# Merged weights of a gated graph network: split halves turned by DMA in place of whole float32 products

## The chip, the cores and the metric

The kernel runs on one core of a Trainium2 chip. The metric is device time in microseconds (us). PE is the matrix engine (TensorE), PEld its weight loads, DVE VectorE, ACT ScalarE, POOL GpSimd, SP the engine that issues most transfers; SPq and ACTq are the queues of DMA-issuing instructions of SP and ACT.

## The reference, cut to what matters

There are B = 16 graphs of N = 512 nodes with D = 128 features. The first part is a gated graph network of L = 5 layers, the same GRU weights in each layer and one `weight[l]` per layer:

```python
for l in range(5):
    m = einsum('bnd,de->bne', h, weight[l])
    agg = einsum('bij,bid->bjd', A, m)
    h = _gru_cell(agg, h, w_ih, w_hh, b_ih, b_hh)   # gi = agg @ w_ih.T + b_ih
x = _layernorm(x + h * mask)
```

The second part is a small graph convolution over the first 25 nodes in five groups, with a softmax of five weights, then another residual and layernorm. It is spread through and behind the first part and matters here only by the tile BD, which holds its block-diagonal adjacency.

## The kernel before, in words

**The merged weights.** The aggregation works on h itself, and `weight[l]` is multiplied into `w_ih` once: WC[l] is `weight[l] @ w_ih.T`, 128 x 384, kept as two float16 halves (high and low part) scaled by 1024. Every float32 product of the network is made of three float16 matmuls: high by high, high by low, low by high (split_product, L783 to L786).

**The steps.** The work is 80 steps k = 0 to 79, one graph and one layer each, in an order written out by hand (ROUNDS, GRAPH, LAYER). Layer 1 appears first at step 4, layer 2 at step 10, layer 3 at step 17, layer 4 at step 25. PE runs, for step k: the aggregation of the *next* step k + 1 (aggregate, L779, 8 matmuls), the gates from the state (gates_of_state, 9 matmuls), then between(k), then the gates from the messages (gates_of_messages, 9 matmuls: R, Z, then IN). In steps 1 and 2 the aggregation of step k + 1 comes last instead of first, so that those of steps 3 and 4 lie next to each other. gates_of_messages waits for wc_lo at the first step of a layer, so step 4 needs WC[1]. ACT makes in each step the high half of the messages (L1145), issues loads, makes the high half of the new state (L1149), then the gates R and Z and the tanh. DVE makes the new state (L1399, L1403), the low half of the messages (L1383), the candidate (L1389, L1393), then prepare(k). POOL makes the low half of the state (state_lo, L526), the kept share Z * H (kept_share, L515), then its own prepare(k). Each engine runs its instructions in the order of the code.

**The turned states.** The aggregation of step t needs the state in natural layout, NAT, which SP makes from the transposed state HT by one DMA transposition of both halves, 128 x 1024 float16 (transpose(t), L400 to L414). SP issues them one behind the other in the order t = 2, 4, 3, 5, 6, ... (L454); the transposition for step 5 waits for the aggregation of step 3 and for the low half of the state of step 1. In the first layer of a graph the same transposition goes from NAT to HT.

**The merge before.** w_ih is turned by PE at the start and stored as WIT; weight[0] too, and WC[0] is merged at once. At step 2, between(2) turns weight[1] to weight[4] by four float32 PE transposes into bank pC (L1000), and DVE's prepare(2) copies the bank to WLT (L1541). At steps 3, 4, 5, 6 between(k) runs merge(k - 2): one float32 matmul with 384 columns (L763, shown by the profile as two), from which ACT takes the high half before its R of the same step (L1138) and DVE the low half in prepare(k) (L1363). All these weights lie in scr, a view of BD; so POOL's prepare(7) waits until the five merges are done and then zeroes BD (L657) and H1 (L658). POOL's prepare(16) (L673 to L675) and DVE's work on degrees follow a chain of their own in steps 13 to 22, which fills BD.

**The loads.** ACT issues in step k, behind the high half of the messages, the loads that tables give: adjacency matrices of 1 MB (load_a, L1116), states x (L1090); in step 3 the matrix of graph 4, in steps 4 to 7 a small corner of all adjacencies (L1097), in step 4 also the matrix of graph 5.

Of the kernel before, what the change touches and what calls it, by code (L numbers as in the profile page):

```python
# [6 lines left out]
ALU = mybir.AluOpType  # L7
ACT = mybir.ActivationFunctionType
# [8 lines left out]
L = 5  # L17
# [11 lines left out]
WARM_UP = 6  # L29
WSCALE = 1024.0  # L30
UNSCALE = 1.0 / WSCALE


ROUNDS = [(0, 1, 2, 3),
# [94 lines left out]
def graph_net_kernel(nc, x, adj, nodemask, weight, w_ih, w_hh, b_ih, b_hh, W1, b1, W2, b2, fusion_w, out):  # L129
    ctx = ExitStack()  # L130
    with ctx:
# [6 lines left out]
        def sem(name):  # L138
            return ctx.enter_context(nc.semaphore(name))
# [66 lines left out]
        WL = scr[:, 6 * D:11 * D].rearrange("p (l e) -> p l e", l=L)  # L206
        WT = scr[:, 11 * D:15 * D]
        WIT = WT[:, 0:3 * D]
        WLT = scr[:, 14 * D:19 * D].rearrange("p (l e) -> p l e", l=L)


        y_flat = Y[:, :, :, :].rearrange("p s i d -> p (s i d)")
# [81 lines left out]
        wh_lo = sem("wh_lo")  # L294
        wi_t = sem("wi_t")
        wi_v = sem("wi_v")
        wl_t = sem("wl_t")
        wl_v = sem("wl_v")
        wc_mm = sem("wc_mm")
        wc_hi = sem("wc_hi")  # L300
        wc_lo = sem("wc_lo")
# [86 lines left out]
        @block.sync  # L388
        def _(sp):
            def load_x(b):  # L390
                if b >= 3:

                    sp.wait_ge(nat_lo, b - 2)
                    sp.wait_ge(x_t, b - 2)
                sp.dma_start(XS[:, b % 3, :, :], x[b, :, :].rearrange("(i p) d -> p i d", p=P)).then_inc(ld_x[b % 3], 16)

            def load_a(b):
                sp.dma_start(AS[:, b % 3, :, :], adj[b, :, :].rearrange("(i p) n -> p i n", p=P)).then_inc(ld_a[b % 3], 16)

            def transpose(t):  # L400
                b = GRAPH[t]
                if LAYER[t] == 0:
                    sp.wait_ge(nat_lo, b + 1)
                    sp.dma_start_transpose(HT[:, b, :, :].rearrange("p h (i n) -> p (h i) n", i=NI),
                                           NAT[:, t % 2, :, :, :].rearrange("p h i d -> p (h i d)"))\
                        .then_inc(turn[t % 2], 16)
                else:
                    sp.wait_ge(ag_mm, t - 1)
                    if LAYER[t - 2] == 0 and t >= 4:
                        sp.wait_ge(turn[t % 2], 16 * ((t - 2) // 2))  # L410
                    sp.wait_ge(h_lo, KEPT[PREV[t]])
                    sp.dma_start_transpose(NAT[:, t % 2, :, :, :].rearrange("p h i d -> p (h i) d"),
                                           HT[:, b, :, :].rearrange("p h n -> p (h n)"))\
                        .then_inc(turn[t % 2], 16)  # L414

            def turn_back(b):

                sp.wait_ge(h_lo, KEPT[FINAL[b]])
                if b < 4:
                    sp.wait_ge(bd_p, BD_STEPS - 1)  # L420
                else:
                    sp.wait_ge(st_y[b % 4], 32 * (b // 4))
                sp.dma_start_transpose(y_halves(b).rearrange("p h i d -> p (h i) d"),
                                       HT[:, b, :, :].rearrange("p h n -> p (h n)")).then_inc(back_t[b % 2], 16)

            def store_y(b):
                sp.wait_ge(f_on, b + 1)
                if E0 <= b < B - 2:
                    sp.wait_ge(f_dn, b - E0 + 1)
                if b >= B - 2:  # L430
                    sp.wait_ge(f_dv, b - B + 3)
                sp.dma_start(out[b, S:P, :], Y[S:P, b % 4, 0, :]).then_inc(st_y[b % 4], 16)
                sp.dma_start(out[b, P:N, :].rearrange("(i p) d -> p i d", p=P),
                             Y[:, b % 4, 1:NI, :]).then_inc(st_y[b % 4], 16)

            def store_z(c):
                sp.wait_ge(g_zo, 1)
                sp.dma_start(out[Q * c:Q * c + Q, 0:S, :], FUB[:, c, :]).then_inc(st_z, 16)

            sp.dma_start(WHS, w_hh.rearrange("(g c) d -> c g d", c=P)).then_inc(ld_wh, 16)  # L440
            sp.dma_start(WI, w_ih.rearrange("(g c) d -> c g d", c=P)).then_inc(ld_wi, 16)
            sp.dma_start(WL[:, 0, :], weight[0, :, :]).then_inc(ld_wi, 16)
            for i in range(NI):
                sp.dma_start(AS[:, 0, i, :], adj[0, i * P:(i + 1) * P, :]).then_inc(ld_a0[i], 16)

            sp.wait_ge(ld_wi, 32)
            load_x(1)
            load_a(1)
            load_x(2)
            load_a(2)  # L450
            load_x(3)
            sp.dma_start(WL[:, 1:L, :], weight[1:L, :, :].rearrange("l d e -> d l e")).then_inc(ld_wl, 16)

            for t in [2, 4, 3, *range(5, K)]:  # L454
                transpose(t)
                for b in range(BY_DMA):
                    if t == FINAL[b] + 4:
                        turn_back(b)
                for b in range(B):
                    if t == FINAL[b] + SCALED[b] + 5:  # L460
                        store_y(b)
            for b in range(B - 4):
                if FINAL[b] + SCALED[b] + 5 >= K:
                    store_y(b)
            for c in range(TAIL):
                store_z(c)
            for b in range(B - 4, B):
                store_y(b)
            for slot in range(4):
                sp.wait_ge(st_y[slot], 32 * (B // 4))  # L470
            sp.wait_ge(st_z, 16 * NC)

        @block.gpsimd
        def _(pool):
# [175 lines left out]
            def prepare(k):  # L650
                if k == 6:
                    pool.wait_ge(fw_x, 1)
                    g_.tensor_tensor(FW[:, :], EC[:, :], FX[:, :], ALU.pow).then_inc(fw_p, 1)
                elif k == 7:

                    pool.wait_ge(wc_mm, L)
                    g_.memset(BD[:, :, :, :, :].rearrange("p g c q s -> p (g c q s)"), 0.0)  # L657
# [90 lines left out]
        def _(pe):  # L748
# [11 lines left out]
                last.then_inc(x_t, 1)  # L760

            def merge(l, bank):
                mm(bank[:, 0:3 * D], WLT[:, l, :], WIT, start=True, stop=True).then_inc(wc_mm, 1)  # L763

            def aggregate(k):
                b = GRAPH[k]
# [122 lines left out]
            def conv_a(c, bank):  # L889
                pe.wait_ge(ag_lo, K)  # L890
                pe.wait_ge(e_x, 1)

                mm(bank[:, 0:COL[1]], X1[:, c, :], BD[:, 0, c, :, :], start=True, stop=True)
                mm(bank[:, COL[1]:COL[G]].rearrange("p (g q n) -> p g q n", g=G - 1, q=Q), X1[:, c, :],
                   BD[:, 1:G, c, :, 0:S // 2], start=True, stop=True).then_inc(c_mm, 1)
# [97 lines left out]
                    mm(pF[:, 0:TAIL * D], SELT, RDB, start=True, stop=True).then_inc(g_mm, 1)  # L993

            def between(k):
                if k == 2:
                    pe.wait_ge(ld_wl, 16)
                    pe.wait_ge(cols_v, 1)
                    for l in range(1, L):
                        last = tr(pC[:, (l - 1) * D:l * D], WL[:, l, :], IDF[:, :])  # L1000
                    last.then_inc(wl_t, 1)
                if 3 <= k < L + 2:
                    l = k - 2
                    if l == 1:
                        pe.wait_ge(wl_v, 1)
                    else:
                        pe.wait_ge(wc_lo, l - 1)
                    merge(l, pF if l % 2 else pC)

            def first_messages():  # L1010
                pe.wait_ge(ld_r, 16 * 4)
# [19 lines left out]
            for k in range(1, K):  # L1031
# [6 lines left out]
                    early_gates()  # L1038
                if k == EARLY + 1:
                    conv_a(TAIL, LAST_BANKS[0])  # L1040
                if 2 < k < K - 1:
                    aggregate(k + 1)
                gates_of_state(k)
# [38 lines left out]
        def _(act):  # L1082
# [53 lines left out]
            def merged_hi(l, bank):  # L1136
                act.wait_ge(wc_mm, l + 1)
                fn(WC[:, l, 0, :, :].rearrange("p g d -> p (g d)"), bank[:, 0:3 * D], ACT.Copy,  # L1138
                   scale=WSCALE).then_inc(wc_hi, 1)

            def aggregated_hi(k):
                act.wait_ge(ag_mm, k + 1)
# [144 lines left out]
            for k in range(1, K):  # L1287
# [16 lines left out]
                        normalise(b)  # L1304
                if SPLIT[k - 1]:
                    state_hi(k - 1)
                if 3 <= k < L + 2:
                    merged_hi(k - 2, pF if (k - 2) % 2 else pC)
                if at := batch_stage(k, 1):
                    batch(at)  # L1310
                if k == EARLY - 1:
# [4 lines left out]
                update_gate(k)  # L1316
                if k == 1:
                    natural_hi(3)
                if EARLY - 1 <= k <= EARLY:
                    masked(E0 + k - EARLY + 1)  # L1320
                if k == EARLY + 1:
# [27 lines left out]
        def _(dve):  # L1349
# [9 lines left out]
                dve.wait_ge(x_hi, t + 1)  # L1359
                v.tensor_tensor(HT[:, t, 1, :], bank[:, :], HT[:, t, 0, :], ALU.subtract).then_inc(x_lo, 1)  # L1360

            def split_lo(dst_hi, dst_lo, bank):
                return v.scalar_tensor_tensor(out=dst_lo, in0=bank[:, 0:3 * D].rearrange("p (g d) -> p g d", g=3),  # L1363
                                              scalar=WSCALE, in1=dst_hi, op0=ALU.mult, op1=ALU.subtract)

            def merged_lo(l, bank):
                dve.wait_ge(wc_hi, l + 1)
                split_lo(WC[:, l, 0, :, :], WC[:, l, 1, :, :], bank).then_inc(wc_lo, 1)

            def cast_first(i):  # L1370
                dve.wait_ge(ld_a0[i], 16)
# [164 lines left out]
                dve.wait_ge(b2_v, 1)  # L1536

            def prepare(k):
                if k == 2:
                    dve.wait_ge(wl_t, 1)  # L1540
                    v.tensor_copy(WLT[:, 1:L, :].rearrange("p l d -> p (l d)"), pC[:, :]).then_inc(wl_v, 1)  # L1541
                if 3 <= k < L + 2:
                    merged_lo(k - 2, pF if (k - 2) % 2 else pC)
                if k == 3:
                    for q in range(Q):
                        v.tensor_copy(ONE[S * q:S * q + S, 1:2], MASK[0:S, E0 + q, 0:1])
# [86 lines left out]
            aggregated_lo(1)  # L1633
            for k in range(1, K):
                new_state(k - 1)
                if k == EARLY:
                    early_state()
                if k == 2:
# [83 lines left out]
```

## Time and profile before

| | |
|---|---|
| median of 3 runs | 494.58 us (494.0 to 495.58) |
| profiled execution, its own time | 494.57 us |
| its span in the trace | 492.8 us |
| PE busy | 482.4 us, 98% of the span |
| DVE busy | 352.5 us, 72% |
| POOL busy | 334.8 us, 68% |
| ACT busy | 303.3 us, 62% |
| mean granted TensorE clock | 0.997 of full speed |
| chain that ended last | PE 82%, POOL 6%, DMA 4%, DVE 3% |

The span runs from the first to the last instruction in the trace; the time of the execution is 1.8 us more. Times of instructions are us from the start of the span. A matmul of 512 columns is shown with 379 ns, but starts of neighbours are 0.216 us apart, since they overlap; what a matmul occupies is read from the chain, not from its shown duration.

### The profile page before, as it was taken

What the parts mean: (1) busy time and instruction counts of PE and PEld (TensorE: products, weight loads), DVE (VectorE), ACT (ScalarE), POOL (GpSimd) and SP (SyncE); (2) the same over time, 40 slices, a digit from 0 to 9 for tenths busy, and PEclk for the clock granted to TensorE, in tenths of its full rate; (3) what the DMA queues carried; (4) which work ended last, traced back from release to release, by engine and by line L of the source; (5) the groups of instructions that cost most, each with busy time, mean ns of one, the idle gap of its engine ahead of it and who ended that gap; (6) DMA issues with size and microseconds to landing.
All of it is one profiled execution on the core that took longest, in us unless ns stands there. A gap on an engine that the chain in (4) does not pass through costs nothing.

```text
span 492.8 us, 7184 instructions
## 1 busy us (share of the span) xinstructions
PE 482.4 (98%) x2305; PEld 230.2 (47%) x2305; DVE 352.5 (72%) x663; ACT 303.3 (62%) x536; POOL 334.8 (68%) x378
## 2 busy tenths in 40 slices
PE   7999999999999999999999999999999999999995
PEld 5344444444444444444444444444444444564564
DVE  3777867696866687778687768868668675445796
ACT  4556655655655566777667776576755767645555
POOL 3654774748775598997689658659996766234466
PEclk9999999999999999999999999999999999999998
DMA  8878252665535447264955486223443233322313
GB/s 269 257 172 159 45 150 55 175 160 129 119 68 156 108 95 185 51 140 105 184 112 154 113 196 179 66 51 82 97 100 75 48 65 67 65 38 44 80 45 86
DMA packets 133732, 55.97 MB, mean 114 GB/s; under 512 B 97257, under 2 KB 125374, under 8 KB 133694
## 3 DMA queue, kind: packets, MB, share of 16 engines
q1 hardware_dynamic: 108316, 32.39, 32.3%
q10 hardware_dynamic: 25378, 23.12, 15.3%
q8 instruction: 18, 0.29, 0.3%
q14 instruction: 20, 0.16, 0.1%
HBM read 27.70 MB, written 4.19 MB: 65 GB/s over the span
## 4 chain that ended last, share of the span: by engine, by line
PE 82%; POOL 6%; DMA 4%; DVE 3%; issue 2%; ACT 2%; SPq 0%; POOLq 0%; DVEq 0%; ACTq 0%
PE pA L779 24%; PE pR L784 6%; PE pR L786 6%; PE pR L785 6%; PE pZ L786 6%; PE pZ L785 6%; PE pZ L784 6%; PE pIN L784 3%; PE pHN L784 3%; PE pIN L786 3%; PE pHN L785 3%; PE pIN L785 3%; PE pHN L786 3%; POOL ZH L515 2%; DMA HT<-NAT 1%
## 5 line engine op out<-in xcount | busy, mean ns | idle before, releaser
L526 POOL TENSOR_TENSOR HT<-H,HT 128x512 f16<-128x512 f32 x76 | 91.8, 1208 | 91.4 <-ACT HT L1149 91.4
L779 PE MATMUL pA<-A,NAT 128*128 128x512 fp8e4 x640 | 151.0, 379 | 0.0
L515 POOL TENSOR_TENSOR ZH<-Z,H 128x512 f32<-128x512 f32 (+1 forms) x80 | 102.6, 1282 | 28.7 <-ACT Z L1164 27.4
L1389 DVE SCALAR_TENSOR_TENSOR T<-pHN,BHN,R 128x512 f32<-128x512 f32 (+1 forms) x80 | 59.9, 748 | 78.5 <-ACT R L1156 78.1
L1169 ACT ACTIVATE pIN<-T,COLS 128x512 f32<-128x512 f32 (+1 forms) x80 | 55.3, 691 | 71.7 <-DVE T L1393 71.6
L779 PEld LDWEIGHTS pA<-A,NAT 128*128 128x128 f16 x640 | 62.3, 98 | 75.3 <-issue 1.5
L1149 ACT ACTIVATE HT<-H 128x512 f16<-128x512 f32 x76 | 47.8, 629 | 64.6 <-DVE H L1403 64.4
L1399 DVE SCALAR_TENSOR_TENSOR pIN<-Z,pIN 128x512 f32<-128x512 f32 (+1 forms) x80 | 55.1, 688 | 24.5 <-ACT pIN L1169 24.3
L1156 ACT ACTIVATE R<-pR,BRZ 128x512 f32<-128x512 f32 (+1 forms) x80 | 54.3, 679 | 22.4 <-PE pR L786 21.5
L1403 DVE TENSOR_TENSOR H<-ZH,pIN 128x512 f32<-128x512 f32 (+1 forms) x80 | 54.8, 685 | 10.0 <-POOL ZH L515 7.6
L1383 DVE TENSOR_TENSOR AG<-pA,AG 128x512 f16<-128x512 f32 x80 | 54.7, 684 | 8.1 <-ACT AG L1145 8.1
L1393 DVE TENSOR_TENSOR T<-pIN,T 128x512 f32<-128x512 f32 (+1 forms) x80 | 55.2, 690 | 3.0 <-PE pIN L786 0.3
L1145 ACT ACTIVATE AG<-pA 128x512 f16<-128x512 f32 x80 | 47.2, 590 | 13.1 <-PE pA L779 9.2
L1164 ACT ACTIVATE Z<-pZ,BRZ 128x512 f32<-128x512 f32 (+1 forms) x80 | 54.5, 682 | 0.0
L784 PE MATMUL pIN<-AG,WC 128*128 128x512 f16 (+1 forms) x80 | 30.4, 380 | 0.6 <-DVE H L1403 0.6
L784 PE MATMUL pR<-AG,WC 128*128 128x512 f16 (+1 forms) x80 | 30.3, 379 | 0.5 <-DVE AG L1383 0.4
L784 PE MATMUL pHN<-HT,WH 128*128 128x512 f16 (+1 forms) x79 | 29.9, 379 | 0.7 <-DMA HT<-NAT 0.7
L786 PE MATMUL pR<-AG,WC 128*128 128x512 f16 (+1 forms) x80 | 30.3, 379 | 0.0
L785 PE MATMUL pZ<-HT,WH 128*128 128x512 f16 (+1 forms) x80 | 30.3, 379 | 0.0
L785 PE MATMUL pZ<-AG,WC 128*128 128x512 f16 (+1 forms) x80 | 30.3, 379 | 0.0
L784 PE MATMUL pZ<-HT,WH 128*128 128x512 f16 (+1 forms) x80 | 30.3, 379 | 0.0
L786 PE MATMUL pIN<-AG,WC 128*128 128x512 f16 (+1 forms) x80 | 30.3, 379 | 0.0
(288 smaller groups left out, 813.9 us busy)
## 6 DMA issues: line engine op xcount, KB each, us to landing
AS<-in_adj_dram ACTq DMA_DIRECT2D x13, 1024.0 KB, 5.9
XR<-in_x_dram ACTq DMA_DIRECT2D x16, 256.0 KB, 2.9
XS<-in_x_dram ACTq DMA_DIRECT2D x13, 256.0 KB, 3.6
out_dram<-Y SPq DMA_DIRECT2D x16, 192.0 KB, 2.3
AS<-in_adj_dram SPq DMA_DIRECT2D x2, 1024.0 KB, 8.8
AS<-in_adj_dram SPq DMA_DIRECT2D x4, 256.0 KB, 5.5
NAT<-HT SPq DMA_TRANSPOSE x64, 3.1
XS<-in_x_dram SPq DMA_DIRECT2D x3, 256.0 KB, 7.8
```

Source lines behind the costliest of these rows:

```text
L515: g_.tensor_tensor(ZH[:, cs], Z[:, cs], H[:, b, cs], ALU.mult).then_inc(zh_p, 1)
L526: g_.tensor_tensor(HT[:, b, 1, :], H[:, b, :], HT[:, b, 0, :], ALU.subtract).then_inc(h_lo, 1)
L779: last = mm(pA2[:, k % 2, :], NAT[:, k % 2, h, i, :], A8[:, b, i, :], start=(h == 0 and i == 0), stop=(h == 1 and i == NI - 1))
L784: mm(bank, w_hi, v_hi, start=start, stop=False)
L785: mm(bank, w_hi, v_lo, start=False, stop=False)
L786: return mm(bank, w_lo, v_hi, start=False, stop=stop)
L1169: fn(pIN[:, cs], T[:, cs], ACT.Tanh, bias=BI[:, 2:3], scale=UNSCALE).then_inc(n_a, 1)
L1383: v.tensor_tensor(AG[:, k % 2, 1, :], pA2[:, k % 2, :], AG[:, k % 2, 0, :], ALU.subtract).then_inc(ag_lo, 1)
L1389: v.scalar_tensor_tensor(out=T[:, cs], in0=pHN[:, cs], scalar=BHN[:, 0:1], in1=R[:, cs], op0=ALU.add, op1=ALU.mult).then_inc(t_v, 1)
L1393: v.tensor_tensor(T[:, cs], pIN[:, cs], T[:, cs], ALU.add).then_inc(u_v, 1)
L1399: v.scalar_tensor_tensor(out=pIN[:, cs], in0=Z[:, cs], scalar=1.0, in1=pIN[:, cs], op0=ALU.subtract, op1=ALU.mult).then_inc(e_v, 1)
L1403: v.tensor_tensor(H[:, GRAPH[k], cs], ZH[:, cs], pIN[:, cs], ALU.subtract).then_inc(h_v, 1)
```

## The change

It does the following:

- ACT and DVE split WIT (step 1) and weight[1] to weight[4] in their natural layout (step 2) into float16 halves scaled by 1024: two ACT casts, two DVE instructions.
- SP turns the eight 128 x 128 halves of the four weights by one DMA transposition of 128 x 1024 float16. It stands in SP's order behind the transposition for step 3 and ahead of that for step 5, and waits for the second DVE instruction (wl_lo).
- PE's four transposes and DVE's copy at step 2 go. The merges of layers 1 to 4 are three float16 matmuls of 384 columns each, and run in steps 4, 5, 6, 7: the first at the start of step 4, ahead of the aggregation of step 5, the others where they were, one step later.
- ACT takes the high half of merge(1) in step 4, where merge(2) was; DVE takes the low half right behind the new state in step 4. The results are scaled back by 1/1024.
- POOL zeroes BD and H1 at step 15 in place of step 7.

```diff
--- before.py
+++ after.py
@@ -29,6 +29,8 @@
 WARM_UP = 6
 WSCALE = 1024.0
 UNSCALE = 1.0 / WSCALE
+
+MERGED = [WSCALE] + [UNSCALE] * (L - 1)
 
 
 ROUNDS = [(0, 1, 2, 3),
@@ -206,7 +208,11 @@
         WL = scr[:, 6 * D:11 * D].rearrange("p (l e) -> p l e", l=L)
         WT = scr[:, 11 * D:15 * D]
         WIT = WT[:, 0:3 * D]
-        WLT = scr[:, 14 * D:19 * D].rearrange("p (l e) -> p l e", l=L)
+        WLT0 = scr[:, 14 * D:15 * D]
+
+        WLN = scr[:, 0:4 * D].bitcast(F16).rearrange("p (h l e) -> p h l e", h=2, l=L - 1)
+        WIF = scr[:, 4 * D:7 * D].bitcast(F16).rearrange("p (h e) -> p h e", h=2)
+        WLF = scr[:, 15 * D:19 * D].bitcast(F16).rearrange("p (h l e) -> p h l e", h=2, l=L - 1)
 
 
         y_flat = Y[:, :, :, :].rearrange("p s i d -> p (s i d)")
@@ -294,8 +300,11 @@
         wh_lo = sem("wh_lo")
         wi_t = sem("wi_t")
         wi_v = sem("wi_v")
+        wi_hi = sem("wi_hi")
+        wi_lo = sem("wi_lo")
+        wl_hi = sem("wl_hi")
+        wl_lo = sem("wl_lo")
         wl_t = sem("wl_t")
-        wl_v = sem("wl_v")
         wc_mm = sem("wc_mm")
         wc_hi = sem("wc_hi")
         wc_lo = sem("wc_lo")
@@ -452,6 +461,10 @@
             sp.dma_start(WL[:, 1:L, :], weight[1:L, :, :].rearrange("l d e -> d l e")).then_inc(ld_wl, 16)
 
             for t in [2, 4, 3, *range(5, K)]:
+                if t == 5:
+                    sp.wait_ge(wl_lo, 1)
+                    sp.dma_start_transpose(WLF[:, :, :, :].rearrange("p h l e -> p (h l) e"),
+                                           WLN[:, :, :, :].rearrange("p h l e -> p (h l e)")).then_inc(wl_t, 16)
                 transpose(t)
                 for b in range(BY_DMA):
                     if t == FINAL[b] + 4:
@@ -651,7 +664,7 @@
                 if k == 6:
                     pool.wait_ge(fw_x, 1)
                     g_.tensor_tensor(FW[:, :], EC[:, :], FX[:, :], ALU.pow).then_inc(fw_p, 1)
-                elif k == 7:
+                elif k == 15:
 
                     pool.wait_ge(wc_mm, L)
                     g_.memset(BD[:, :, :, :, :].rearrange("p g c q s -> p (g c q s)"), 0.0)
@@ -760,7 +773,14 @@
                 last.then_inc(x_t, 1)
 
             def merge(l, bank):
-                mm(bank[:, 0:3 * D], WLT[:, l, :], WIT, start=True, stop=True).then_inc(wc_mm, 1)
+                if l == 0:
+                    mm(bank[:, 0:3 * D], WLT0, WIT, start=True, stop=True).then_inc(wc_mm, 1)
+                    return
+                pe.wait_ge(wl_t, 16)
+                pe.wait_ge(wi_lo, 1)
+                pe.wait_ge(wc_lo, l)
+                split_product(bank[:, 0:3 * D], WLF[:, 0, l - 1, :], WLF[:, 1, l - 1, :], WIF[:, 0, :], WIF[:, 1, :],
+                              True, True).then_inc(wc_mm, 1)
 
             def aggregate(k):
                 b = GRAPH[k]
@@ -993,19 +1013,8 @@
                     mm(pF[:, 0:TAIL * D], SELT, RDB, start=True, stop=True).then_inc(g_mm, 1)
 
             def between(k):
-                if k == 2:
-                    pe.wait_ge(ld_wl, 16)
-                    pe.wait_ge(cols_v, 1)
-                    for l in range(1, L):
-                        last = tr(pC[:, (l - 1) * D:l * D], WL[:, l, :], IDF[:, :])
-                    last.then_inc(wl_t, 1)
-                if 3 <= k < L + 2:
-                    l = k - 2
-                    if l == 1:
-                        pe.wait_ge(wl_v, 1)
-                    else:
-                        pe.wait_ge(wc_lo, l - 1)
-                    merge(l, pF if l % 2 else pC)
+                if 5 <= k < L + 3:
+                    merge(k - 3, pF if (k - 3) % 2 else pC)
 
             def first_messages():
                 pe.wait_ge(ld_r, 16 * 4)
@@ -1038,6 +1047,10 @@
                     early_gates()
                 if k == EARLY + 1:
                     conv_a(TAIL, LAST_BANKS[0])
+                if k == 4:
+
+                    pe.wait_ge(cols_v, 1)
+                    merge(1, pF)
                 if 2 < k < K - 1:
                     aggregate(k + 1)
                 gates_of_state(k)
@@ -1136,7 +1149,7 @@
             def merged_hi(l, bank):
                 act.wait_ge(wc_mm, l + 1)
                 fn(WC[:, l, 0, :, :].rearrange("p g d -> p (g d)"), bank[:, 0:3 * D], ACT.Copy,
-                   scale=WSCALE).then_inc(wc_hi, 1)
+                   scale=MERGED[l]).then_inc(wc_hi, 1)
 
             def aggregated_hi(k):
                 act.wait_ge(ag_mm, k + 1)
@@ -1304,8 +1317,8 @@
                         normalise(b)
                 if SPLIT[k - 1]:
                     state_hi(k - 1)
-                if 3 <= k < L + 2:
-                    merged_hi(k - 2, pF if (k - 2) % 2 else pC)
+                if 4 <= k < L + 3:
+                    merged_hi(k - 3, pF if (k - 3) % 2 else pC)
                 if at := batch_stage(k, 1):
                     batch(at)
                 if k == EARLY - 1:
@@ -1316,6 +1329,10 @@
                 update_gate(k)
                 if k == 1:
                     natural_hi(3)
+                    fn(WIF[:, 0, :], WIT, ACT.Copy, scale=WSCALE).then_inc(wi_hi, 1)
+                if k == 2:
+                    act.wait_ge(ld_wl, 16)
+                    fn(WLN[:, 0, :, :], WL[:, 1:L, :], ACT.Copy, scale=WSCALE).then_inc(wl_hi, 1)
                 if EARLY - 1 <= k <= EARLY:
                     masked(E0 + k - EARLY + 1)
                 if k == EARLY + 1:
@@ -1359,13 +1376,13 @@
                 dve.wait_ge(x_hi, t + 1)
                 v.tensor_tensor(HT[:, t, 1, :], bank[:, :], HT[:, t, 0, :], ALU.subtract).then_inc(x_lo, 1)
 
-            def split_lo(dst_hi, dst_lo, bank):
+            def split_lo(dst_hi, dst_lo, bank, scale=WSCALE):
                 return v.scalar_tensor_tensor(out=dst_lo, in0=bank[:, 0:3 * D].rearrange("p (g d) -> p g d", g=3),
-                                              scalar=WSCALE, in1=dst_hi, op0=ALU.mult, op1=ALU.subtract)
+                                              scalar=scale, in1=dst_hi, op0=ALU.mult, op1=ALU.subtract)
 
             def merged_lo(l, bank):
                 dve.wait_ge(wc_hi, l + 1)
-                split_lo(WC[:, l, 0, :, :], WC[:, l, 1, :, :], bank).then_inc(wc_lo, 1)
+                split_lo(WC[:, l, 0, :, :], WC[:, l, 1, :, :], bank, MERGED[l]).then_inc(wc_lo, 1)
 
             def cast_first(i):
                 dve.wait_ge(ld_a0[i], 16)
@@ -1536,11 +1553,16 @@
                 dve.wait_ge(b2_v, 1)
 
             def prepare(k):
+                if k == 1:
+                    dve.wait_ge(wi_hi, 1)
+                    v.scalar_tensor_tensor(out=WIF[:, 1, :], in0=WIT, scalar=WSCALE, in1=WIF[:, 0, :],
+                                           op0=ALU.mult, op1=ALU.subtract).then_inc(wi_lo, 1)
                 if k == 2:
-                    dve.wait_ge(wl_t, 1)
-                    v.tensor_copy(WLT[:, 1:L, :].rearrange("p l d -> p (l d)"), pC[:, :]).then_inc(wl_v, 1)
-                if 3 <= k < L + 2:
-                    merged_lo(k - 2, pF if (k - 2) % 2 else pC)
+                    dve.wait_ge(wl_hi, 1)
+                    v.scalar_tensor_tensor(out=WLN[:, 1, :, :], in0=WL[:, 1:L, :], scalar=WSCALE, in1=WLN[:, 0, :, :],
+                                           op0=ALU.mult, op1=ALU.subtract).then_inc(wl_lo, 1)
+                if 5 <= k < L + 3:
+                    merged_lo(k - 3, pF if (k - 3) % 2 else pC)
                 if k == 3:
                     for q in range(Q):
                         v.tensor_copy(ONE[S * q:S * q + S, 1:2], MASK[0:S, E0 + q, 0:1])
@@ -1633,6 +1655,8 @@
             aggregated_lo(1)
             for k in range(1, K):
                 new_state(k - 1)
+                if k == 4:
+                    merged_lo(1, pF)
                 if k == EARLY:
                     early_state()
                 if k == 2:
```

## Rows read from the trace of the kernel before

**Rows 1.** Windows: us, busy of PE, PEld, DVE, ACT, POOL, then clock, DMA share, GB/s.

```profile
144.00:480.00 336.00, 335.00 (x1609) 158.44 (x1607) 241.42 (x455) 214.97 (x387) 234.12 (x277) 1.00 0.44 100
```

**Rows 2.** Chain that ended last, steps 2 and 3: start, us, what.

```profile
24.99 0.44 PE pC L1000 x4
...
32.77 0.65 PE pF L763 x2
```

**Rows 3.** Timeline of PE, steps 2 to 4: start, us, what.

```profile
26.56 0.38 PE L784 MATMUL pIN<-AG,WC 128*128 128x512 f16 x1
...
35.19 1.89 PE L779 MATMUL pA<-A,NAT 128*128 128x512 fp8e4 x8
...
38.86 0.81 PE L763 MATMUL pC<-BD 128*128 128x384 f32 x2
```

**Rows 4.** Timeline of DVE, steps 2 and 3.

```profile
24.89 0.69 DVE L1403 TENSOR_TENSOR H<-ZH,pIN 128x512 f32<-128x512 f32 x1
...
29.77 0.69 DVE L1383 TENSOR_TENSOR AG<-pA,AG 128x512 f16<-128x512 f32 x1 [1.44 <-ACT AG L1145]
30.37 0.68 DVE L1541 COPY BD<-pC 128x512 f32<-128x512 f32 x1
...
36.21 0.55 DVE L1363 SCALAR_TENSOR_TENSOR WC<-pF,WC 128x384 f16<-128x384 f32 x1
```

**Rows 5.** Timeline of SP's queue: when transpositions were issued.

```profile
17.13 1.34 SPq L404 DMA_TRANSPOSE HT<-NAT  x1
...
29.13 1.23 SPq L412 DMA_TRANSPOSE NAT<-HT  x1
34.35 1.23 SPq L412 DMA_TRANSPOSE NAT<-HT  x1
```

**Rows 6.** DMA issues of windows at 17.1, 29.1, 34.4, 61.5 us: last number, us to landing.

```profile
HT<-NAT SPq DMA_TRANSPOSE x1, 5.7
...
NAT<-HT SPq DMA_TRANSPOSE x1, 3.0
...
NAT<-HT SPq DMA_TRANSPOSE x1, 4.6
...
NAT<-HT SPq DMA_TRANSPOSE x1, 6.6
```

**Rows 7.** Timeline of ACT and its queue, steps 1 to 4.

```profile
16.34 0.40 ACTq L1116 DMA_DIRECT2D AS<-in_adj_dram  x1
...
31.26 0.45 ACTq L1116 DMA_DIRECT2D AS<-in_adj_dram  x1
...
37.52 0.45 ACTq L1116 DMA_DIRECT2D AS<-in_adj_dram  x1
39.51 0.63 ACT L1149 ACTIVATE HT<-H 128x512 f16<-128x512 f32 x1 [1.79 <-DVE H L1403]
40.05 0.47 ACT L1138 ACTIVATE WC<-pC 128x384 f16<-128x384 f32 x1
```

**Rows 8.** Windows around PE's last matmul, columns as in rows 1.

```profile
487.00:488.00 1.00, 0.19 (x2) 0.00 (x0) 0.73 (x6) 0.43 (x2) 0.81 (x1) 1.00 0.19 49
...
490.00:491.00 1.00, 0.00 (x0) 0.00 (x0) 0.00 (x0) 0.00 (x0) 0.00 (x0) 0.56 0.33 79
```

**Rows 9.** Timeline of POOL, steps 7 and 15.

```profile
62.46 2.23 POOL L657 MEMSET BD<- 128x2560 f32 x1
64.62 1.17 POOL L658 MEMSET H<- 128x1280 f32 x1
...
105.83 1.27 POOL L515 TENSOR_TENSOR ZH<-Z,H 128x512 f32<-128x512 f32 x1
...
109.72 1.48 POOL L526 TENSOR_TENSOR HT<-H,HT 128x512 f16<-128x512 f32 x1 [2.62 <-ACT HT L1149]
```

**Rows 10.** Timeline of DVE and of PE's weight loads at step 17.

```profile
120.02 0.69 DVE L1403 TENSOR_TENSOR H<-ZH,pIN 128x512 f32<-128x512 f32 x1 [0.58 <-POOL ZH L515]
...
120.76 0.10 PEld L784 LDWEIGHTS pIN<-AG,WC 128*128 128x128 f16 x1 [0.32 <-DVE H L1403]
```

## The prediction

> **What bounds the kernel now.** I read the busy windows first. From 144 to 480 us PE is busy 335.00 of 336.00 us at full granted clock [rows 1], and the timeline of PE shows the same from about 24 us on, so a microsecond taken from PE there, or added as a wait, goes fully into the time. No other engine is near it (VectorE 72%). In this regime a change of the kind made here can give only what it takes off PE, and costs whatever it makes PE wait; work on ACT, DVE, POOL and SP counts only where it makes PE late. So the timelines of steps 2 to 4 and 15 to 17 decide, and in them what PE's next instruction waits for.
>
> **Part 1: PE's own work.** The four float32 transposes of step 2 occupy PE for 0.44 us and one float32 merge for 0.65 us [rows 2]. Four merges and the transposes are 4 x 0.65 + 0.44 = 3.04 us. In their place stand 12 float16 matmuls of 384 columns. A 512-column one takes 1.73 / 8 = 0.216 us of PE's chain (the aggregation of eight; section on the profile: starts 0.216 us apart), so 384 columns are 0.162 us, three 0.49 us, twelve 1.94 us. Gain: **1.1 us**. This is all that the change can give.
>
> **Part 2: the insertions of steps 1 and 2.** Two ACT casts go where ACT waited for DVE's candidate; they cost nothing while that idle time stands, half a microsecond each without it. On DVE the low half of w_ih (128 x 384, priced by the merge's low half, 0.55 us) comes ahead of the new state of step 1. That state was ready at 24.89 + 0.69 = 25.58 [rows 4] and now is at 26.13. PE's IN matmul that needs it stood at 26.56 [rows 3] and moves up by the 0.44 us of transposes to 26.12: a wait of 0 to 0.1 us, taken as nothing. The low half of the four weights takes the place of the copy (0.68 us), at about the same price: nothing.
>
> **Part 3: when the weights are turned.** DVE's low half of the messages of step 3 started at 29.77 and the copy 0.60 behind it [rows 4]. With the 0.55 us inserted in step 1, DVE now reaches the weights' low half at about 30.9 and ends it at 31.5. Only then may SP issue the new transposition. Behind it on SP's queue stands the transposition for step 5, which before was issued at 29.13 [rows 5]; it now goes out one issue (1.23 us) later than the new one, at 32.75. That is a move of 3.6 us.
>
> How long does it take to land? The row for 29.13 says 3.0 us, with no load beside it. But ACT issues the 1 MB matrix of graph 4 at 31.26 [rows 7], or about 30.8 when PE is 0.44 us earlier, so 0.7 us ahead of the new transposition. Transpositions beside such a load landed after 5.7 us (issued at 17.13, load at 16.34), 4.6 (issued at 34.35, 3.1 us behind the load) and 6.6 us (at 61.49) [rows 5 to 7]. The nearest is 5.7, since its load had the same lead. So the weights land at 37.2 and the transposition for step 5 at 38.4; ends 34.5 and 35.75 (3.0 us), 38.1 and 39.35 (6.6 us).
>
> **Part 4: PE at step 4.** Aggregation 5 started at 35.19 [rows 3]. Transposes and the merge of step 3 are gone ahead of it, so PE is there at 35.19 - 0.44 - 0.65 = 34.1 and finds merge(1). It waits 3.1 us for the weights, computes 0.49 us, waits 0.7 us more for the turned state of step 5. The aggregation starts at 38.4 and the **wait is 38.4 - 34.1 - 0.49 = 3.8 us** (ends 1.15 and 4.75). Queued behind this wait on PE is everything: aggregation, gates, and through them ACT's and DVE's steps. What is late next is not another load; those are issued behind ACT's messages and shift along.
>
> **Part 5: WC[1] in the same step.** The messages' gates of step 4 need both halves of WC[1]. PE is there 38.86 - 35.19 = 3.67 us behind the aggregation's start [rows 3]. On ACT the high half stands behind the next messages' high half, the load issues (done 37.52 + 0.45 - 35.19 = 2.78 us behind the same point), the state's high half (0.54 us to the next start) and takes 0.47 [rows 7]; with DVE's 0.55 [rows 4] that ends at 4.35. **Wait 0.7 us** (0.3 to 0.9). Before, the merge of layer 1 had a whole step for this.
>
> **Part 6: the zeroing.** At step 7 it takes 2.23 + 1.17 us of POOL and PE lost nothing there; its leaving gives nothing. At step 15 POOL's kept share ends at 105.83 + 1.27 = 107.1, and its next work starts at 109.72 [rows 9]. The idle 2.6 us don't hold 3.4: state_lo starts at 110.4, 0.7 us late. Behind it POOL has no pause through step 16 (pow on degrees) to the share of step 17. There DVE's new state is released by POOL, at 120.02, ends at 120.71, and PE's IN weights already wait 0.32 us for it [rows 10]. So nothing absorbs the shift: **0.6 us** (0 to 0.7).
>
> **Sum:** -1.1 + 3.8 + 0.7 + 0.6 = **+4.0 us**. The profiled execution took 494.57 us (span 492.8 and 1.8 around it), practically the median of 494.58. Forecast 498.6.
>
> **The clock.** PE's last matmul ended at 487.2 and the granted clock stood at 1.00 then, but averages 0.56 over 490 to 491 [rows 8]: it fell from 2.4 to 1.2 GHz about 3 us after PE stopped. The wait in part 4 is two pieces, 3.1 and 0.7 us, with 0.5 us of matmuls between, so it comes just to that point. No row with matmuls at the lower level stands in this trace. The Trainium skill (TensorE: Matmul & The Clock Gate, Part 1) says that a PE left waiting on transfers falls back to half clock and starts its next work cold; by it the sum would be the higher one of the second rival. What the return costs: if PE needs as long to come back as it took to fall, an estimate from rows 8, 3 us at half speed lose 1.5 us.
>
> **The rivals.** A change within 0.3% (1.5 us) can't be told from none for this kernel.
>
> - *Forecast*, 0.60: both transpositions land beside the load. With 4.6 us for them it is 497.6, with 6.6 us 499.6; without the zeroing 0.6 less. Own range 497.0 to 499.6.
> - *The clock falls too*, 0.17: 498.6 + 1.5 = 500.1, up to 501.1. For: the wait is as long as what made it fall at the end. Against: the matmuls between the pieces, and a wait that may be shorter.
> - *The load doesn't disturb*, 0.08: landing in 3.0 us, wait 1.15: 494.57 - 1.1 + 1.15 + 0.7 + 0.6 = 495.9, or 495.3. For: the load's own data may come later than its issue. Against: three rows beside loads.
> - *The cover holds (not slower)*, 0.10: the halves are ready early enough that the weights have landed by 34.1 and the state by 34.6. Then only -1.1 is left, 493.5, with a zeroing that hides. It decides at a DVE end of about 29.9 even at 3.0 us a transposition with 1.23 us between them; DVE's order in steps 1 and 2 puts the end at 31.5. I see nothing that would bring it 1.6 us forward, unless the two overlap more in landing or PE was held elsewhere.
> - *The float16 merges are no cheaper*: then 0.65 us more on any of these; no case of its own. The remaining 0.05 is for what I don't see.
>
> **The numbers.** The likeliest case gives 498.6. The range 496.0 to 501.0 leaves out the cover that holds (0.10), part of the undisturbed landing and the rest: just under 2 in 10. Faster by over 0.3% (under 493.1) would need more than all the PE work removed: 0.03. Within 0.3%: the cover case and part of the short landing, 0.13. Slower: 0.84.
>
> **What the changed profile would show.** Right: PE idle for 3 to 4 us near 34 to 38, released by the two transpositions of SP; the new one issued at 31 to 32 and landing near 5.7 us later; a wait of 0.7 us on DVE's WC ahead of R at step 4; the IN matmuls of step 18 held 0.6 us longer by DVE's state; three merge matmuls in 0.49 us. The rest of PE's timeline back to back as before. Wrong: SP issuing the new transposition before 30 us; both landing within 3 to 4 us with the load beside them; a granted clock under 1 behind the wait; POOL's state_lo of step 15 on time.

## The result and the profile after

The changed kernel takes 507.14 us (median of 5 runs, 504.65 to 507.87) against 494.58 us before: ratio 1.0234, 95% interval 1.0214 to 1.0255. Slower was forecast, but by 4.0 us; it is 12.6, outside the range of 496.0 to 501.0.

The first part of the profile's page after, and its slices of PE's clock:

```profile
span 505.4 us, 7192 instructions
PE 484.3 (96%) x2305; PEld 229.1 (45%) x2305; DVE 358.4 (71%) x664; ACT 303.7 (60%) x538; POOL 335.4 (66%) x378
...
PEclk9997999999999999999999999999999999999999
```

The span grew by 12.6 us and PE's busy time by only 1.9, although 1.1 us of its work is gone. So the time is in waits, and some of PE's work ran slower: one slice of the clock is a 7.

The waits of PE in the changed kernel (engine, line, what it waited for: us in total, times, longest):

```profile
PE pF L804 <- issue: 5.0, 1, 5.0
PE pIN L804 <- DVE H L1420: 4.7, 5, 2.6
...
PE pA L799 <- DVE A L1394: 1.2, 2, 0.6
PE pR L804 <- DVE AG L1400: 0.8, 2, 0.4
PE pR L804 <- DVE WC L1380: 0.6, 1, 0.6
```

The first is merge(1) at step 4 (this row names no releaser), the last the wait for WC[1] in the same step, which the prediction had at 0.7. The second line has three new entries: PE's IN matmuls of steps 2, 16 and 18, which waited for the states of steps 1, 15 and 17. The third line and half of the fourth are new too, but lie in the first 20 us. The timeline of PE shows the places of the others:

```profile
28.58 0.39 PE L804 MATMUL pIN<-AG,WC 128*128 128x512 f16 x1 [1.24 <-DVE H L1420]
...
36.39 0.38 PE L806 MATMUL pIN<-AG,WC 128*128 128x512 f16 x1
41.75 0.48 PE L804 MATMUL pF<-BD 128*128 128x384 f16 x1 [4.98 <-issue]
...
42.67 3.48 PE L799 MATMUL pA<-A,NAT 128*128 128x512 fp8e4 x8
...
48.73 0.39 PE L804 MATMUL pR<-AG,WC 128*128 128x512 f16 x1 [0.64 <-DVE WC L1380]
...
121.72 0.39 PE L804 MATMUL pIN<-AG,WC 128*128 128x512 f16 x1 [2.59 <-DVE H L1420]
...
133.45 0.39 PE L804 MATMUL pIN<-AG,WC 128*128 128x512 f16 x1 [0.34 <-DVE H L1420]
```

The aggregation of step 5 occupied PE for 1.73 us before and is shown with 1.89 [rows 3]; here it is shown with 3.48. The issues of transfers beside it (last number: us to landing), from the windows at 33.5 and at 35.3 us:

```profile
AS<-in_adj_dram ACTq DMA_DIRECT2D x1, 1024.0 KB, 6.5
XS<-in_x_dram ACTq DMA_DIRECT2D x1, 256.0 KB, 7.1
BD<-BD SPq DMA_TRANSPOSE x1, 7.8
...
NAT<-HT SPq DMA_TRANSPOSE x1, 7.2
```

The transposition of the weights, issued at 33.86, landed at 41.7; that of step 5, issued at 35.28, at 42.5. [rows 6] had 5.7 and 6.6 us as the longest beside a load. And the clock, in windows of 1 us (columns as in [rows 1]):

```profile
38.00:39.00 1.00, 0.00 (x0) 0.00 (x0) 0.92 (x6) 0.64 (x1) 0.42 (x1) 1.00 0.83 287
39.00:40.00 1.00, 0.00 (x0) 0.00 (x0) 0.93 (x3) 0.00 (x0) 0.00 (x0) 0.53 1.17 308
...
45.00:46.00 1.00, 1.00 (x5) 0.31 (x3) 0.00 (x0) 0.00 (x0) 0.00 (x0) 0.56 0.00 0
46.00:47.00 1.00, 1.00 (x6) 0.48 (x5) 0.00 (x0) 0.60 (x1) 0.00 (x0) 1.00 0.00 0
```

PE stopped at 36.8; the granted clock fell to 1.2 GHz at about 39.1 and came back at about 45.9, 4.1 us after PE had begun again.

What held DVE at steps 1 and 15 is seen when DVE's timeline

```profile
25.74 1.46 DVE L1558 SCALAR_TENSOR_TENSOR BD<-BD 128x384 f16<-128x384 f32 x1
...
115.95 4.38 DVE L1394 TENSOR_SCALAR A<-AS 128x1024 fp8e4<-128x1024 f32 x1
120.26 0.68 DVE L1416 SCALAR_TENSOR_TENSOR pIN<-Z,pIN 128x512 f32<-128x512 f32 x1
```

is laid beside POOL's:

```profile
25.63 1.16 POOL L517 TENSOR_TENSOR H<-HT 128x512 f32<-128x512 f16 x1
...
115.25 1.27 POOL L528 TENSOR_TENSOR ZH<-Z,H 128x512 f32<-128x512 f32 x1
116.45 2.24 POOL L670 MEMSET BD<- 128x2560 f32 x1
118.62 1.17 POOL L671 MEMSET H<- 128x1280 f32 x1
```

The low half of w_ih (L1558) has 0.55 us of work (seen in e8 below) and ends 0.4 us behind POOL's sum. The cast of half an adjacency, L1394, took 1.11 us at this place in the kernel before, and its other half takes 0.69 us one step later; at step 15 it is shown from 115.95 to 120.33 and ends 0.5 us behind POOL's zeroing. The new state stands behind it on DVE and PE behind that.

### The profile page after: what moved, and what is told of

Read it like the earlier page. It is cut to its first block, busy times and chain, and to the rows that moved or that the text cites. A ratio compares the mean times of both kernels' runs of the same rounds, so it can differ in the third digit from the quotient of the medians.

```text
span 505.4 us, 7192 instructions
## 1 busy us (share of the span) xinstructions
PE 484.3 (96%) x2305; PEld 229.1 (45%) x2305; DVE 358.4 (71%) x664; ACT 303.7 (60%) x538; POOL 335.4 (66%) x378
## 4 chain that ended last, share of the span: by engine, by line
PE 73%; DVE 8%; POOL 7%; issue 4%; DMA 3%; ACT 3%; SPq 0%; ACTq 0%; POOLq 0%; DVEq 0%
PE pA L799 22%; PE pR L804 5%; PE pR L805 5%; PE pR L806 5%; PE pZ L806 5%; PE pZ L804 5%; PE pZ L805 5%; PE pIN L804 3%; PE pIN L805 3%; PE pIN L806 3%; PE pHN L804 3%; PE pHN L806 3%; PE pHN L805 3%; POOL ZH L528 2%; DMA AS<-in_adj_dram 2%
## 5 line engine op out<-in xcount | busy, mean ns | idle before, releaser
L799 PE MATMUL pA<-A,NAT 128*128 128x512 fp8e4 x640 | 152.8, 382 | 1.2 <-DVE A L1394 1.2
L528 POOL TENSOR_TENSOR ZH<-Z,H 128x512 f32<-128x512 f32 (+1 forms) x80 | 102.6, 1283 | 29.9 <-ACT Z L1177 28.3
L804 PE MATMUL pIN<-AG,WC 128*128 128x512 f16 (+1 forms) x80 | 30.4, 380 | 4.7 <-DVE H L1420 4.7
L1394 DVE TENSOR_SCALAR A<-AS 128x1024 fp8e4<-128x1024 f32 x30 | 30.8, 1035 | 0.9 <-DMA AS<-in_adj_dram 0.9
```

Of the source, the lines that this page charges most:

```text
L528: g_.tensor_tensor(ZH[:, cs], Z[:, cs], H[:, b, cs], ALU.mult).then_inc(zh_p, 1)
L799: last = mm(pA2[:, k % 2, :], NAT[:, k % 2, h, i, :], A8[:, b, i, :], start=(h == 0 and i == 0), stop=(h == 1 and i == NI - 1))
L804: mm(bank, w_hi, v_hi, start=start, stop=False)
```

## The experiments

Theory A, after these rows: (1) the 1 MB load issued just ahead of the weights' transposition stretches the landing and so the wait; (2) a wait that long lets the clock fall, which costs by itself; (3) DVE instructions that read and write SBUF are held while POOL works, so the zeroing at step 15 and w_ih's low half cost more than their work. Its rivals are those of the expectations: the landing is the transposition's own, the lower clock is hidden, POOL is only late.

**e0_again**, no edit.

> The changed kernel once more. In its first profile the second aggregation starts 1.57 us later than before (21.86 against 20.29 us), ahead of anything that the change touches except ACT's and DVE's order. If that is chance of the loads, it is not there again, or is there in the kernel before too; if it belongs to the change, it is there in each profile. The wait at merge(1) should again be 4 to 5.5 us and the fall of the granted clock should be there.

507.11 us (505.99 to 507.58; before 494.65 on that chip; ratio 1.0245, 1.0228 to 1.0262). The transposition landed after 7.8 us again, the wait at merge(1) was 5.02 us, and half clock lasted from 39.5 to 46.4, so that the wait for WC[1] was hidden. The late start of the first profile was not the same: the gates of step 2 began at 23.36 us, against 23.76 in the first profile and 22.88 before. The profiles of e5 and e6 below, with the same code up to step 2, begin there at 22.98 and 22.91. So up to 0.9 us of the first profile's 12.6 is chance in the first 20 us. A second fall of the clock, from 121.4 to 124.9, came behind the wait for the state of step 15; the first profile has that wait, of the same length, and no fall.

**e1_zero7**, from the changed kernel:

```diff
-                elif k == 15:
+                elif k == 7:
```

> The changed kernel with the zeroing of BD and H1 back in step 7. Theory A (the zeroing of 3.4 us on POOL holds DVE's cast of the adjacency of graph 7, which took 4.38 us in place of 1.1, so PE waits 2.6 us for the state of step 15 and 0.3 us for that of step 17): faster than the changed kernel by 2.6 to 3.0 us, about 504.3. Theory B (as in the prediction: POOL is only late by 0.7 us at state_lo): faster by 0.6 us.

503.01 us, 4.1 less than e0. The waits for the states of steps 15 and 17 are gone. That is more than theory A gave. The profiles say where it lies: between steps 16 and 19 (start of R's first matmul from the messages) PE loses 4.45 us against before in e0, 3.28 in the first profile, which has the same wait for the state of step 15 but not the second fall of the clock, and 0.02 here. So the second fall costs 1.2 us.

**e3_before_zero15**, the kernel before with only the zeroing moved:

```diff
-                elif k == 7:
+                elif k == 15:
```

> The kernel before with the zeroing alone moved from step 7 to step 15. Theory A (DVE's cast held by POOL's zeroing): slower than before by 2.6 to 3.0 us, 497.3, with the cast at step 15 at about 4.4 us. Theory B (POOL late only): slower by 0.6 us, 495.2, cast at 1.1 us.

499.23 us, ratio 1.0090 (1.0073 to 1.0107), so 4.6 us slower for this one edit, where theory A gave 2.6 to 3.0. DVE and POOL in its timelines:

```profile
106.90 4.38 DVE L1377 TENSOR_SCALAR A<-AS 128x1024 fp8e4<-128x1024 f32 x1
```

```profile
107.40 2.23 POOL L657 MEMSET BD<- 128x2560 f32 x1
109.56 1.17 POOL L658 MEMSET H<- 128x1280 f32 x1
```

The cast took 4.38 us again, PE waited 2.58 us for the state of step 15 and 0.34 for that of step 17. The profiled run, with a mean clock of 0.998 and no fall, took 498.17; the other three had 0.994 to 0.995 and took 499.2 to 499.4. So the clock probably fell in them, at some 1.1 us; they have no profile. That a wait of 2.6 us sometimes lets it fall is seen in e0.

**e4_zero15_cast17**, e3 with the cast out of the way:

```diff
-CAST_AT = {... 7: 15, ...}
+CAST_AT = {... 7: 17, ...}
```

> The kernel before with the zeroing in step 15, as in e3, and DVE's cast of graph 7 moved from steps 15 and 16 to 17 and 18. Theory A (the cast is held while POOL zeroes, and DVE's new state stands behind it): the wait of 2.6 us at step 15 and what follows from it go, only POOL's lateness of 0.3 to 0.6 us at step 17 stays: 495.0 to 495.4. Theory C (the zeroing harms in another way, through transfers or POOL's queue): stays near 499.

495.82 us, ratio 1.0023 (1.0012 to 1.0033): 1.1 us over before, where 0.3 to 0.6 was expected. 3.5 of the 4.6 us are gone by moving the cast. This is part (3) shown for the cast: same zeroing, same place. What is left in its profile is 0.3 us ahead of step 16 and 0.75 between steps 16 and 19. The latter is PE's wait for the state of step 17, the lateness of POOL that the prediction had:

```profile
121.79 0.39 PE L784 MATMUL pIN<-AG,WC 128*128 128x512 f16 x1 [0.57 <-DVE H L1403]
```

**e2_load2**, from the changed kernel:

```diff
-LOAD_A_AT = {4: 3, ...}
+LOAD_A_AT = {4: 2, ...}
```

> The changed kernel with the 1 MB adjacency of graph 4 issued in step 2 in place of step 3, some 7 us ahead of the weights' transposition. If the load beside it is what made the transposition land after 7.8 us: it lands after 3 to 4.5 us, that for step 5 about 1.3 us later, PE waits 1 to 2 us in place of 5, the granted clock does not fall (that alone some 2 us), and the kernel is 5 to 6 us faster, about 501.5. If the landing is the transposition's own: no difference beyond 1 us.

502.99 us, 4.1 less than e0 where 5 to 6 was expected, but 499.38 to 506.27 over four runs. The profiled run (499.38) had the landing after 4.2 us, with the 256 KB load still beside it, waits of 1.09 us at merge(1) and 0.20 behind it, and no fall of the clock. It also made a new wait: the load now lay beside the transposition for step 4, and PE waited 0.96 us for that. The other runs had mean clocks of 0.990 to 0.994 against 0.996, so the clock probably fell in them; which wait let it fall wasn't seen. For part (1) the profile speaks, the median does not.

**e6_zero7_load4**, e1 with the load on the other side, behind both transpositions:

```diff
-                elif k == 15:
+                elif k == 7:
...
-LOAD_A_AT = {4: 3, ...}
+LOAD_A_AT = {4: 4, ...}
```

> The changed kernel with the zeroing back in step 7 and the load of graph 4's adjacency issued in step 4, behind both transpositions, in place of step 3. If the load beside them is what stretches the landing to 7.8 us: landing 3 to 4.5 us, wait at merge(1) and the aggregation together 0.5 to 2 us, clock at 1.00, 496.5 to 498.5. If the transposition of the weights is slow by itself: landing near 7.8 us again and 502 to 503.

497.21 us (496.78 to 497.86), ratio 1.0048 (1.0035 to 1.0061). 5.8 us less than e1 for moving one load by a step; in the profiles 4.6 of them lie between steps 3 and 8, where the edit acts, and 1.1 ahead of step 3, where it can't. The windows of its transfers at 32.3 and 33.7 us:

```profile
XS<-in_x_dram ACTq DMA_DIRECT2D x1, 256.0 KB, 3.3
BD<-BD SPq DMA_TRANSPOSE x1, 3.8
...
NAT<-HT SPq DMA_TRANSPOSE x1, 3.3
```

Part (1) is shown: the 256 KB load is still issued 0.54 us ahead of the transposition, and without the 1 MB load it lands after 3.8 us in place of 7.8. What remains on PE:

```profile
27.06 0.39 PE L804 MATMUL pIN<-AG,WC 128*128 128x512 f16 x1 [0.74 <-DVE H L1420]
...
36.26 0.32 PE L804 MATMUL pF<-BD 128*128 128x384 f16 x1 [1.01 <-issue]
37.06 1.90 PE L799 MATMUL pA<-A,NAT 128*128 128x512 fp8e4 x8 [0.16 <-DMA NAT<-HT]
...
42.11 0.39 PE L804 MATMUL pR<-AG,WC 128*128 128x512 f16 x1 [1.20 <-DVE WC L1380]
```

3.1 us of waits less 1.1 us of work are 2.0; measured 2.5. The wait for WC[1] is longer than in the changed kernel, since ACT now issues one more load ahead of its high half.

**e5_warm**, from the changed kernel, PE kept busy inside its wait:

```diff
                     pe.wait_ge(cols_v, 1)
+                    for _ in range(20):
+                        mm(pF[:, :], WH[:, 0, 0, :], HT[:, 0, 0, :], start=True, stop=True)
                     merge(1, pF)
```

> The changed kernel with 20 extra matmuls of 512 columns (4.3 us at full clock, results overwritten by the merge) on PE just ahead of merge(1), inside its wait of 5 us. If the fall of the clock has a cost of its own: no fall at step 4, aggregation in 1.7 us in place of 3.3 to 3.5, faster than the changed kernel by 1.5 to 3 us, 504 to 505.5. If the lower clock is hidden under other waits: no difference.

504.47 us (504.46 to 505.11), 2.6 less than e0, with 4.3 us more work on PE. The weights land no earlier (7.8 us). Its PE at step 4:

```profile
39.87 0.34 PE L804 MATMUL pF<-BD 128*128 128x384 f16 x1 [0.65 <-DMA BD<-BD]
40.73 1.90 PE L799 MATMUL pA<-A,NAT 128*128 128x512 fp8e4 x8 [0.20 <-DMA NAT<-HT]
...
45.22 0.39 PE L804 MATMUL pR<-AG,WC 128*128 128x512 f16 x1 [0.64 <-DVE WC L1382]
```

The clock stays at this place, the aggregation is back at its old length, and the wait for WC[1] shows again. Part (2) is shown. Its price is read better from the profiles than from the medians, since the start differs, and the clock fell behind step 15 in this profile too (from 118.2 to 121.6). From the start of merge(1) to the aggregation of step 6 it is 7.30 us here, 8.94 in the changed kernel, 9.06 in e0 and 8.40 in e1: the fall costs 1.6, 1.8 and 1.1 us on top of the wait. In this profile the releaser of merge(1) is named too, the transposition BD<-BD.

**e8_wif**, e6 with w_ih's halves made in step 0:

```diff
             merged_hi(0, pIN)
+            fn(WIF[:, 0, :], WIT, ACT.Copy, scale=WSCALE).then_inc(wi_hi, 1)
...
             transposed_lo(1, pF)
+            dve.wait_ge(wi_hi, 1)
+            v.scalar_tensor_tensor(out=WIF[:, 1, :], in0=WIT, scalar=WSCALE, in1=WIF[:, 0, :],
+                                   op0=ALU.mult, op1=ALU.subtract).then_inc(wi_lo, 1)
             cast_half(1, 0)
```

with the two instructions taken out of step 1.

> e6 (zeroing in step 7, load in step 4) with w_ih's halves made in step 0, DVE's low half in the idle time ahead of its cast of graph 1, where POOL does nothing. Theory A (this DVE instruction took 1.46 us in step 1 since POOL was at work on its own tiles beside it, and the state behind it was late for PE by 0.3 to 1.2 us): it takes 0.55 us here, the wait of the IN matmul in step 2 goes, 0.5 to 0.8 us faster than e6. Theory C (1.46 us is what it costs wherever it stands): no gain, a later cast.

The instruction takes 0.55 us there, in a stretch where POOL does nothing (POOL's work ends at 14.0 and begins again at 16.9), and the wait of the IN matmul in step 2 is gone:

```profile
15.43 0.55 DVE L1649 SCALAR_TENSOR_TENSOR BD<-BD 128x384 f16<-128x384 f32 x1
```

From the gates of step 2 to the aggregation of step 5 it is 38.41 - 25.08 = 13.33 us, against 37.06 - 22.91 = 14.15 in e6: 0.8 less, as expected. The times don't show it: 497.12 us, ratio 1.0045 (1.0027 to 1.0063). On that chip before itself took 495.04 and spread from 494.58 to 498.51, and this profile started 2 us late on PE. So theory A is confirmed by the trace for this instruction too, and the gain in time is not resolved.

**e7_early**, the changed kernel with everything earlier: merges, their halves and the zeroing in the steps of before, w_ih's halves as in e8 (but directly behind the biases on DVE), and

```diff
                 if k == 2:
+                    dve.wait_ge(wl_hi, 1)
+                    v.scalar_tensor_tensor(out=WLN[:, 1, :, :], in0=WL[:, 1:L, :], ...).then_inc(wl_lo, 1)
                     cast_half(3, 0)
```

with the high half in ACT's step 1.

> The changed kernel with its split work moved earlier: w_ih's halves in step 0, the four weights' high half on ACT in step 1, their low half on DVE at the start of step 2 behind the new state, merges, their halves and the zeroing in the steps of the kernel before (3 to 6, and 7). The transposition of the weights should be issued near 27 us and land near 31, ahead of the merge of step 3, so PE waits for none of it and only the 1.1 us of PE's work are saved: 493.5. If another wait is made (the candidate of step 2 comes 0.7 us later on DVE): up to 495.

494.29 us (493.82 to 496.86), ratio 0.9995 (0.9984 to 1.0005): no difference. The transposition is issued at 26.89, lands after 3.1 us, and PE waits for none of it. The 1.1 us are given back to two casts that stand behind the new DVE instructions (0.26 and 0.45 us on PE) and a start 0.55 us later (gates of step 2 at 23.43).

**e9_early2**, e7 with those two moved: w_ih's low half as in e8, the weights' low half behind the casts of graph 3.

> e7 with its two DVE instructions moved out of PE's way: w_ih's low half behind the second transposed state in step 0, the four weights' low half behind the casts of graph 3 in step 2. In e7's profile PE waited 0.26 and 0.45 us for casts behind them. Expected: these waits gone, PE waits for no transposition of the weights (issued near 27.6, landing near 31), 0.4 to 1.1 us faster than before, 493.6 to 494.2. If the casts' waits come from the loads: 494.3 as e7.

494.16 us against 495.04 before on the same chip, ratio 0.9979 (0.9961 to 0.9996). Its profile has no wait on PE that before has not, from 22.89 us on, and its span is 491.8 us against 492.8 before. The last step's R matmul from the messages starts at 475.45 against 476.58, 1.13 us earlier. The interval only just leaves out no change; the 0.9 us of the medians agree with this and with the 1.1 us of PE's work.

## Why the prediction was wrong

The direction was right, and so were the two waits at step 4 and their order. Part 6 failed most: it let the zeroing cost only POOL's lateness, 0.6 us, where it cost 3.3 to 4.45 through DVE's cast. Part 2 took a wait at nothing, parts 3 and 4 had the landing too short, and the fall of the clock was left out of the sum.

- **Part 1** held. The three matmuls of a new merge start 0.16 us apart and occupy PE for 0.48 us (54.36, 54.52, 54.68, then the gates at 54.84), against 0.49, and e9 shows what the work alone is worth: 1.13 us on PE against 1.1.
- **Part 2** failed: "0 to 0.1 us, taken as nothing". DVE's insertion was priced by an instruction that reads PSUM (0.55 us). This one reads two operands from SBUF while POOL does, and took 1.46. The state was late for PE by 0.32 to 1.24 us in the profiles of the changed kernel, e0, e1, e2, e5 and e6, 1.24 in the first; e8 shows the same instruction at 0.55.
- **Parts 3 and 4**: the mechanism was right, the term mis-sized. The landing was taken at 5.7 us, upper end 6.6; it was 7.8 in four profiles (the changed kernel, e0, e1, e5). The rows of 5.7 and 6.6 had one load beside them; here a second load (256 KB) was issued at the same moment. The trace of before has it too, 0.49 us behind the 1 MB load (31.75), and the prediction left it out. Alone beside the transposition it leaves 3.8 to 4.2 us (e6, e8, e2). Whether together with the 1 MB load it makes the last 1 to 2 us wasn't tried. The weights were issued at 33.9 and not at 31.5, but PE came later as well, 2.9 us behind the issue against 2.6. The later landing also swallowed the 0.7 us for step 5's state, which landed within the merge. The wait was 5.0 against 3.8.
- **Part 5** held: 0.64 against 0.7.
- **Part 6** failed: "The idle 2.6 us don't hold 3.4 ... 0.6 us". That part of it is right, e4 still has it (0.57 us). What was overlooked is that another engine works beside the zeroing, which was moved into the microseconds of DVE's cast. e3 prices the move at 4.6 us, e4 takes 3.5 of them away; on PE it is 3.3 us, and 4.45 where the clock falls. The prediction asked only whether POOL had room.
- **The clock**, a rival with 0.17 and left out of the sum, was the case. Against it stood that the wait was in two pieces; it came in one. Its price, 1.5 us, was near: 1.6, 1.8 and 1.1, since the clock stayed low for 4.1, 6.0 and 3.0 us behind the restart, against 3. What failed is the step that took the two pieces for a protection. And it falls a second time behind step 15 in some runs, at 1.2 us, which no case of the prediction had.
- **The cover case** names a DVE end of 29.9. By its own times (state landed by 34.6 after 3.0 us, issued 1.23 us behind the weights) it is 30.4. No number of the forecast hangs on it.

The sum, from medians (before took 494.65 us beside e0 and e1, 494.74 beside e6): of some 12.5 us, 4.1 are the zeroing (e0 to e1), 5.8 the load beside the transpositions with the clock it lets fall (e1 to e6; 4.6 by the profiles), 2.5 the remaining waits of 3.1 us less 1.1 of saved work. Against the forecast, the first profile is 8.6 us too long: 2.7 are the zeroing (3.3 against 0.6), 1.2 the wait for the weights, 1.6 the clock, 1.2 the state of step 1, 1.1 came ahead of the messages' gates of step 2, and 0.8 stay without a place. Not settled: the runs of e2 from 502.6 to 506.3, and the start of PE's first 20 us, which differs by up to 2 us between profiles.

## What to carry to other kernels

When an instruction is moved on one engine, look at what the engines beside it do in those microseconds: here a zeroing that POOL had nearly the room for cost 4.6 us, 3.5 of them by one cast on DVE and the clock that fell behind it. Where PE is the bound, price a wait on a transfer twice, once for the landing beside the loads issued just ahead of it (3.1 us with no load issued just ahead, 3.8 to 4.2 beside 256 KB, 7.8 beside 1.25 MB) and once for the clock if PE stands still that long (5.0 us let it fall in all three profiles here, 2.6 us in two of four). Work taken off PE is worth having only where its preparation has slack before the first use; e9 issued the same transposition 5 us earlier, put the zeroing back into step 7, and turned +12.5 us into about -0.9.

## What the runs showed of the hardware

- **DVE beside POOL.** A cast of float32 to fp8 within SBUF took 4.38 us while POOL zeroed, in the changed kernel and in e3, and ended 0.5 us behind the zeroing; the half in the next step took 0.7 us. It was shown from 115.95, while POOL's kept share ran (115.25 to 116.52), and waited behind both zeroings although the first of them started only at 116.45. A DVE instruction with two SBUF operands took 1.46 us beside a POOL instruction that reads SBUF, 0.55 without one (e8). The zeroing (2.24 us, 2.23 in step 7 of before) and POOL's sum (1.16 us, 1.15 before) took no longer for it: here one side waits. The Trainium skill (SBUF — State Buffer, SBUF: two separate sides) says just that of the port pair shared by DVE and GpSimd: an exclusive lock for a whole instruction, not a sharing of bandwidth, for DVE's two-port modes and, against a GpSimd instruction that reads SBUF, its two-input forms. These rows agree, 4.38 us against 0.7 and 1.46 against 0.55. It gives the pair to the side that starts first; the rows at 116 us don't show that, since the zeroing went ahead of a cast that already waited.
- **The clock.** It fell from 2.4 to 1.2 GHz 2.3 us (changed kernel), 4.2 us (e0) and 4.6 us (e1) after PE stopped at step 4, and came back 4.1, 6.0 and 3.0 us after PE was busy again. Behind the wait of 2.6 us in e0 it fell only when PE had been at work again for 1.0 us. The account of the Trainium skill (TensorE: Matmul & The Clock Gate, Part 1), PE falling back on transfer waits and starting cold, agrees for step 4; the price here is 1.1 to 1.8 us, and 20 needless matmuls in the wait bought it back (e5).
- **The transposition beside loads.** 128 x 1024 float16 within SBUF landed after 3.1 us (e7) and 3.2 us (e9) with no load issued in the 3 us ahead of it, 3.8 (e6), 4.2 (e8) and 4.2 us (e2) beside 256 KB, 7.8 us beside 1 MB and 256 KB (changed kernel, e0, e1, e5).
